# State space layer of a twelve-layer decoder: products for the next layer placed on free steps, two vector steps of delta widened to 2048 columns, and a small product of the normalisation by scalars

## The reference, cut to what matters

```
u, z    = split(x @ W_in.T)                    # 512 + 512 channels
u       = silu(causal_conv(u, 4 taps) + b)
dbc     = u @ Wx.T ; dt, B, C = split(dbc)     # 64, 16, 16
delta   = softplus(dt @ Wdt.T + bdt)
h[t]    = exp(delta * A) * h[t-1] + delta * B * u     # 16 states, scan over 256 steps
y       = sum_n h[n] * C[n] + u * D
out     = 0.5 * (y_forward + y_backward) * silu(z) @ W_out.T
```

## Time and profile before

| | |
|---|---|
| median of 3 runs | 4097.02 us (4095.62 to 4098.72) |
| the profiled execution | 4095.32 us, its span 4093.5 us |
| granted TensorE clock, mean | 0.955 of full |
| busy over the span | PE 3697.4, DVE 3043.0, ACT 2288.3, POOL 1358.1 us |
| loop of the state space layer | from 70.8 to 1074.9 us |
| DVE in that stretch | 889.51 us busy of 1004.10 |
| POOL in that stretch | 864.65 us busy |

### The profile page before, as it was taken

The page is one execution under the profiler, slowest core; times in us unless marked ns, Lnnn a source line. Parts: engine busy times, 40 slices in busy tenths (PEclk is TensorE's granted clock), DMA queues, the critical chain, the costliest instruction groups (busy, mean ns, idle before and its releaser), DMA issues. The chain is left out here.

```text
span 4093.5 us, 57650 instructions
## 1 busy us (share of the span) xinstructions
PE 3697.4 (90%) x20026; PEld 2576.0 (63%) x20026; DVE 3043.0 (74%) x7078; ACT 2288.3 (56%) x5545; POOL 1358.1 (33%) x873
## 2 busy tenths in 40 slices
PE   5787888988899989999999998788898889889998
PEld 2344334344466668997888896555566558645787
DVE  6889988988787667667888786677577774465777
ACT  5676676766565532223555557677687652253446
POOL 3989888897400000000332323366321200010000
PEclk8998998999899999999999999889999999999999
DMA  4454554656532000000000001000000000100000
GB/s 125 147 160 149 167 173 152 182 170 207 203 94 64 29 24 21 21 22 14 1 1 1 1 1 43 15 1 1 13 2 1 20 24 1 43 0 21 1 1 21
DMA packets 144152, 239.57 MB, mean 59 GB/s; under 512 B 23303, under 2 KB 66831, under 8 KB 141175
## 3 DMA queue, kind: packets, MB, share of 16 engines
q1 hardware_dynamic: 113187, 211.96, 16.7%
q10 hardware_dynamic: 30676, 23.93, 1.8%
HBM read 209.29 MB, written 26.54 MB: 58 GB/s over the span
## 5 line engine op out<-in xcount | busy, mean ns | idle before, releaser
L1274 DVE TENSOR_TENSOR_SCAN db<-PS,db 128x512 f32<-128x512 f32 x512 | 592.5, 1205 | 65.4 <-ACT PS L1239 45.2
L209 PE MATMUL PS<-db,cst 128*128 128x512 f32 x1024 | 500.0, 628 | 37.0 <-DVE db L1279 36.9
L216 PE MATMUL PS<-cst,p 128*128 128x128 f32 (+1 forms) x2880 | 397.4, 284 | 45.5 <-DVE pt L3509 15.6
L216 PEld LDWEIGHTS PS<-cst,p 128*128 128x128 f32 (+1 forms) x2880 | 333.0, 148 | 117.9 <-issue 55.1
L2249 POOL TENSOR_TENSOR rb<-rb,tb 128x512 f32<-128x512 f32 x32 | 42.9, 1343 | 1095.3 <-DVE tb L2244 1095.3
L209 PEld LDWEIGHTS PS<-db,cst 128*128 128x128 f32 x1024 | 204.4, 203 | 296.1 <-issue 233.4
L209 PE MATMUL PS<-xnT,W 128*128 128x256 f32 (+2 forms) x880 | 324.3, 511 | 47.2 <-ACT tt L1093 16.8
L1220 POOL TENSOR_TENSOR db<-W,b 128x1024 f32<-128x1024 f32 x128 | 312.0, 2464 | 31.8 <-PE PS L209 31.6
L1220 POOL TENSOR_TENSOR db<-du,b 128x1024 f32<-128x1024 f32 x128 | 303.1, 2391 | 45.3 <-PE PS L209 44.8
L209 PEld LDWEIGHTS PS<-xnT,W 128*128 128x128 f32 (+1 forms) x880 | 168.1, 196 | 178.4 <-issue 119.1
L2100 ACT ACTIVATE W<-PS,W 128x512 f32<-128x512 f32 x144 | 98.8, 690 | 288.6 <-PE PS L209 270.4
(11 more groups left out here) (467 smaller groups left out, 8474.0 us busy)
## 6 DMA issues: line engine op xcount, KB each, us to landing
b<-bc_rows SPq DMA_DIRECT2D x256, 256.0 KB, 3.7
c<-bc_rows SPq DMA_DIRECT2D x256, 256.0 KB, 4.0
qk<-fore_qk SPq DMA_DIRECT2D x48, 294.5 KB, 3.0
fore_qk<-W ACTq DMA_DIRECT2D x48, 256.0 KB, 4.4
W<-in_we SPq DMA_DIRECT2D x9, 1024.0 KB, 4.8
W<-in_w SPq DMA_DIRECT2D x48, 128.0 KB, 3.9
fore_v<-W ACTq DMA_DIRECT2D x24, 256.0 KB, 3.2
v<-fore_v SPq DMA_DIRECT2D x6, 1024.0 KB
```

The costliest lines, as they stand in the source:

```text
L209: ins = T.matmul(out, l, r, start=first and i == 0, stop=last and i == len(pairs) - 1)
L216: ins = T.transpose(bank[0:m, c:c + r], s, ident[0:r, 0:r])
L1274: V.tensor_tensor_scan(db[:, f, r], self.ring.PS[:, self.BANKS[x % 3], r], db[:, f, r], 0.0, ALU.mult, ALU.add).then_inc(self.sc.sem, 1)
```

## The change: what it does

1. `dve_scale`: one SCALAR_TENSOR_TENSOR on 128x4 becomes four TENSOR_SCALAR on 128x1, whose scalars are one column of rs and -1.
2. For k above 0, MAX is one instruction over 2048 columns at step 10 of the plan, and ADD one over 2048 columns at step 14. It now waits for both of POOL's SUB pieces; the pieces at steps 15 and 16 do nothing. k = 0 is as before.
3. OUT and ADDX of a chunk stand at consecutive steps 71 to 75 and 72 to 76 (of 64c) in place of every second step from 75 and 76.
4. The norm of the third chunk starts at step 204 in place of 211.
5. `Fore` has four spans of steps in place of START and APART. A step is free where PE has no piece (a GATE counts only where j is even, an OUT where j < 4) and where (i-2) mod 32 is above 2, which leaves out the step of `dve_y` and the two after it, now in the last chunk too. The 28 or 24 products of a run are spread evenly over the free steps of its span.

```
 dve_scale
-        V.scalar_tensor_tensor(ms, mv[:, :, 0], -1.0, rs, ALU.mult, ALU.mult).then_inc(self.rs.sem, 1)
+        for j in range(4):
+            ins = V.tensor_scalar(ms[:, j:j + 1], mv[:, j, 0:1], rs[:, j:j + 1], -1.0, ALU.mult, ALU.mult)
+        ins.then_inc(self.rs.sem, 1)
 Mamba.setup
-                self.todo[64 * c + 75 + 2 * j].append((self.OUT, c, j))
-                self.todo[64 * c + 76 + 2 * j].append((self.ADDX, c, j))
+                self.todo[64 * c + 71 + j].append((self.OUT, c, j))
+                self.todo[64 * c + 72 + j].append((self.ADDX, c, j))
-        self.nxt.early, self.nxt.brisk = {0: 83, 1: 147, 2: 211}, (2,)
+        self.nxt.early, self.nxt.brisk = {0: 83, 1: 147, 2: 204}, (2,)
+    @classmethod
+    def on_pe(cls, what, k, j):
+        return j % 2 == 0 if what == cls.GATE else what == cls.OUT and j < 4 or what == cls.READY and j in cls.ON_PE
 dve_piece, MAX
-            t1, t2, dl = [split(a, 2)[:, r, :] for a in (self.t1, self.t2, delta)]
+            if k and r:
+                return
+            t1, t2, dl = [split(a, 2)[:, r, :] if k == 0 else a for a in (self.t1, self.t2, delta)]
 dve_piece, ADD
-            r = j - self.ADD
-            t1, t2, dl = [split(a, 2)[:, r, :] for a in (self.t1, self.t2, delta)]
-            e.wait_ge(e.own, e.ups)
-            e.wait_ge(*self.sp_(2 * k + r - 1))
-            V.tensor_tensor(dl, t2, t1, ALU.add).then_inc(self.dls.sem, 1)
+            if j == self.ADD:
+                e.wait_ge(e.own, e.ups)
+                e.wait_ge(*self.sp_(2 * k))
+                V.tensor_tensor(delta, self.t2, self.t1, ALU.add).then_inc(self.dls.sem, 2)
 Fore
-    CHUNKS, START, APART, LATEST, GAIN = 3, (7, 102, 166, 222), (2, 1, 1, 1), 6, 4
+    CHUNKS, SPANS, LATEST, GAIN = 3, ((7, 101), (102, 165), (166, 217), (217, 255)), 6, 4
-        free = [i for i in range(len(todo)) if i >= 224 or not any(
-            x[0] in (Mamba.GATE, Mamba.OUT) or x[0] == Mamba.READY and x[2] in Mamba.ON_PE for x in todo[i])]
+        free = [i for i in range(len(todo)) if (i - 2) % 32 > 2 and not any(Mamba.on_pe(*x) for x in todo[i])]
-        for i, s in enumerate(self.START):
-            steps = []
-            for x in free:
-                if x >= (steps[-1] + self.APART[i] if steps else s):
-                    steps.append(x)
-            self.steps += steps[:self.early if i == 0 else 24]
+        for i, (lo, hi) in enumerate(self.SPANS):
+            k, at = self.early if i == 0 else 24, [x for x in free if lo <= x < hi]
+            self.steps += [at[j * len(at) // k] for j in range(k)]
```

## The result

The changed kernel takes 4073.3 us (median of 7 runs, 4061.5 to 4078.4) against 4097.0 in 7 runs of the kernel before taken beside it. The ratio is 0.9931, 95% interval 0.9905 to 0.9956: 0.7% faster, where 4079 was forecast (0.44%) with a range of 4064 to 4103. The profiled execution took 4063.6 us, span 4061.8. From the first scan to the last the loop took 1002.9 us before and 965.5 now. The other eleven layers follow unchanged.

What follows compares the result with a forecast made beforehand. DVE and POOL were nearly full in the loop, the loss mainly DVE's waits, some 95 us. Terms summing to -18.1 us, put against the median 4097.0, gave 4079 us, range 4064 to 4103.

Steps and rivals of the forecast that it cites:

- A: DVE's wait for PE's last sums at steps 34, 194, 226: moving early products off saves their own time, 7.2 us.
- B: Last chunk, 978 to 1038 us, PE fully busy: fewer early products there remove DVE's six waits for POOL, 4.9 us saved.
- C: Wait for ACT behind the Silu at step 220: the third norm's affine map moves to step 212, 2.0 us saved.
- D: DVE's additions waiting for PE's output products: with no early products between these, 4 of 5.1 us saved.
- E: Second chunk's dense steps 118 to 127: freeing some steps shortens DVE's waits for POOL, 2 us saved, bounds 0 and 6.
- H: Early products moved beside the Silu each add an ACT copy of 0.58 us, five times: 3 us lost, 0 to 4.
- G: Wide MAX and ADD: 11 to 14 us more DVE time, mostly absorbed; 2 us lost, bounds -4 and +14.
- rival (a): Delta's wide ADD is on the path and nothing absorbs it: +13 us in place of +2, 4090 us; chance 0.16.
- F: Norm's product as four small instructions, twelve times: 3 us saved, between 2.6 lost and 5.7 saved.
- Rival (c): In six norm pieces the four scalar instructions each lose the race to POOL: 42 us added, 4124 us; chance 0.10.
- Rival (b): Loop's gaps move to the next engine's queue and don't vanish; a quarter of the gain stays, 4093 us; chance 0.11.

Runs made afterwards that it cites:

- put_back: The changed kernel with five early products back on the steps of the gate's wait (32, 34, 194, 224, 226); ratio to the kernel before 0.9922, 4077.3 us at equal clock.
- spread_only: The kernel before with only changes 3, 4 and 5 (norm product and delta as they were); ratio 0.9884, 4077.1 us at equal clock.
- all_but_wide: The changed kernel with MAX and ADD in halves as before; ratio to the kernel before 0.9926, 4075.8 us at equal clock.
- max_wide: The changed kernel with MAX wide but ADD in two halves at steps 14 and 16; ratio to the kernel before 0.9886, 4066.9 us at equal clock.
- outs_only: The kernel before with only the output products and their additions at consecutive steps; ratio 1.0000, 4096.7 us at equal clock.
- thinned: max_wide with nine dense early-product steps left out and the last two spans changed; ratio to the kernel before 0.9904, 4073.1 us at equal clock.
- wide_only: The kernel before with only MAX and ADD made wide (2048 columns); ratio 0.9978, 4103.4 us at equal clock.
- control: The kernel before, unchanged, run once more for its trace; loop 992.2 us against 1002.9 in the first trace.
- excl_only: The kernel before with early products only kept off the dve_y step and the two behind it; ratio 0.9969, 4094.1 us at equal clock.
- probes: The changed kernel with one extra small DVE instruction per loop step, six forms in turn; TENSOR_SCALAR on 128x1 never took more than 0.214 us.

## Why the prediction was right, and where it was not

The time lies 6 us under the forecast and in the range; faster had 0.68. Its sum of -18 met a measured -24 (medians), -26 to -27 (equal clock) and -34 (loop, two traces each). That the loop's gain comes off the total one for one is borne out: the stretch behind the loop is as long as before at the same late clock. So the mechanisms were mostly found, and the sum was little more than half of the loop's gain; that the medians came within 6 us of 4079 is in part luck. Two bounds were off: the low end of the range took 4 us for the second chunk where its own favourable bound is 6 (4062, not 4064), and the 8 us that a measurement was to tell from no change are narrower than the interval measured, which is 10 us to either side.

- **A, gate's wait, -7.2.** Measured -13.1. The step that failed is "what I leave standing is that the sums themselves come late": the whole wait went at 34, 194 and 226. At 226 the wait goes with the products on every step ahead of it, which spreading thinned; at 194 nothing ahead was thinned, and the cause is open. put_back shows that the products' own time, on which my term rested, is right for step 34 (2.33 us) and that they cost nothing at the other two.
- **B, last chunk, -4.9.** Right: five waits of 0.8 us and one of 1.0 are gone, PE is at 94%.
- **C, third norm, -2.0.** Right in place; 4.93 became 3.31, so -1.6; in the three kernels with ADD in halves and the norm at step 204 (spread_only, all_but_wide, max_wide) it became 2.96, the full 2.0.
- **D, OUT and ADDX, -4.** Wrong in the changed kernel: -0.8. Alone (outs_only) the waits do go from 5.1 to 0.2 us, yet the time stays. I had read a wait as a gain without asking what the moved products meet next.
- **E, second chunk, -2.** About -1: the waits at steps 124 to 130 sum to 6.1 and 4.1 before, 4.9 and 3.2 after. The dense run is still there; thinned took it away.
- **H, +3.** Nothing: the waits behind Silu are 2.96 us as before; that the copies fit into ACT's own waits there is a guess. And a term was missing: the waits for ACT fell by 11.4 us in all. C's 1.6 are among them. Steps 59, 123 and 187 lose 1.3, 1.3 and 0.8 us; spread_only keeps these (1.1, 1.2, 0.8) and wide_only doesn't (0.3, 0.5, 0), so they are the wide MAX; that ACT has caught up behind it, a wait turned into DVE's work, is how I read it. Step 48 loses 2.0, and this goes with the gate's wait at step 34: 4.60, 3.42, 3.04, 2.03 and 2.02 us (before, control, put_back, excl_only, changed) where step 34 waited 3.55, 2.32, 2.33, 1.29 and nothing. It isn't the copies of the products just ahead, which are the same in excl_only as before. So my term for A also left out what its wait draws behind it. The steps 138 to 140 and 199 to 204 lose some 4; spread_only has this gain too. In those runs early products followed each other before, each with a copy of 0.58 us on ACT; that the copies are the cause is read from the places and wasn't tried apart.
- **G, delta, +2.** ADD was sized right: 41 to 44 us forecast, 28.2 + 16.2 = 44.4 measured, though with a longer wait for SUB (2.3 us in the mean, 1.3 forecast) and the port lost in six of seven only. MAX was sized wrong: 28.6 forecast, 21.3 measured, because I had carried over the 6.11 us that lie in a group of the earlier trace rows and that the control shows to be a lost race, and let the wide form meet as many as the first halves had. Absorption was right at the steps named (the waits at 18, 82 and 146 fall from 1.1 to 0.2 us), and for the two merges together: all_but_wide, without them, is no faster, where rival (a) wanted 8 to 14 us. But part of this is MAX's gain. The wide ADD by itself stays in the time with some 6 us (max_wide), so rival (a) had the place right, at half its price.
- **F, norm's product, -3.** It never waits, the better of the two cases; but four take 0.6 us, not the 0.38 of another instruction, so that twelve save 3 us of DVE's time and not 5.7. Alone it gives 8 us, more than was forecast, and its trace explains this only in part: 3.2 us at steps 87 and 151 are its own; on top of the spreading 1 (all_but_wide against spread_only), within the uncertainty. Rival (c) is refuted by the probes: 128x1 never waited for POOL.

Rival (b), the gaps move: it happened to D, and to thinned. It did not to A, and the loop kept more than the sum forecast.

## What to carry to other kernels

A wait for a late engine has two parts: the work right ahead of the awaited piece, and the queue that the engine brought with it; only the second is removed by thinning the neighbours. At step 226 it was the larger (3.8 of 5.85 us stay in excl_only), at step 34 the smaller (2.3 of 3.55 come back in put_back). Work taken off one step has to be given a thin place, or it makes the next engine late somewhere else. Of two merges of vector instructions, the one that stands where its inputs are long ready gains, and the one that now waits for the later of two inputs loses a whole foreign instruction on top. Before a gain of 1% is explained, run the kernel before a second time: here two traces of it differ by 10.7 us in the loop, 7.7 of them by one lost race and a late sum. And before times are compared at equal clock, see whether the change itself has moved the clock.

## What the runs showed of the hardware

- DVE and POOL: a DVE instruction with two arrays from SBUF that starts while POOL works can be passed over more than once. It waited for one (2.05 us, six of seven wide ADD), for three (6.11 in place of 1.32 us) and for five (12.61 us in place of 3.4). A start 0.17 us behind POOL's is enough to lose. What decides how many go ahead is not shown: at the wide ADD of k = 1 DVE got in after one, though POOL had a second at hand.
- TENSOR_SCALAR on 128x1 with one array from SBUF doesn't take part in this (0.18 to 0.216 us in 90 places, 65 of them with a POOL instruction under way); with two elements it does (0.2 to 2.36 us).
- Between runs of one kernel here, 0.001 of the mean granted clock goes with 3.2 us, and the largest part of it is decided in a stretch of 330 us near the end, at 0.99 in one execution and 0.91 in another of the same kernel.
